# Two layers on one core: latent scores of four heads at once on four banks, rounds of exponentials and masks, and new second-layer stages

## The chip, the core and the metric

The kernel runs on one of the eight cores of a Trainium2 chip. The core's engines run their own instruction streams and meet at semaphores: TensorE (PE, matmuls, a 128x128 array), VectorE (DVE), ScalarE (ACT), GpSimd (POOL) and SyncE (SP, which issues most DMAs). Matmuls write to PSUM; here it is split in two tiles of four banks of 512 fp32 columns each, `pA` and `pD`. All arithmetic is fp32. The metric is the device time of one execution in microseconds; lower is better.

## The reference, cut to what matters

```python
x = L0_attn_x                                    # (8, 512, 256)
xn = layernorm(x)
s = retention(xn)                                # 4 heads, chunks of 64
g = silu(local_ffn(xn))                          # DEPTH = 2 layers, below
x = x + s * g
xn = layernorm(x)
s = latent_attention(xn)                         # 16 heads, below
g = silu(moe(xn))                                # 8 experts, top 2, F = 1024
return x + s * g

def local_layer(x):                              # twice
    h = shift_token(x)                           # half of the channels one token back
    q, k, v = split(h @ wqkv)                    # 8 heads of 64
    q, k = xpos(l2norm(q) * qs, l2norm(k) * ks)
    x = x + attention(q, k, v, window=128) @ wo
    h = layernorm(shift_token(x)) * lg + lb
    a, g = split(h @ w1 + b1)
    return x + (a * gelu(g)) @ w2 + b2

def latent_attention(x):                         # per sequence of 512 tokens
    c_q, c_kv = x @ W_DQ, x @ W_DKV              # 64 latent channels
    Q = [c_q @ W_UQ, rope(c_q @ W_QR)]           # 16 heads of 16 + 8
    K = [c_kv @ W_UK, rope(x @ W_KR)]            # the 8 rotary rows shared by all heads
    scores = clip(Q @ K.T, -80, 80)              # causal
    return softmax(scores / sqrt(24)) @ (c_kv @ W_UV) @ W_O
```

## The kernel before

**Stages.** B = 8 sequences, two local layers, so 16 items; `stages()` yields k = -1 to 15. A stage finishes item k (output projection, feed-forward) and starts item k + 1 (q, k, v, scores, probabilities). Stages 0 to 7 also do retention of sequence k; stages 8 to 15 (the upper stages) also do the latent attention of sequence b = k - 8. Stage 15 has no item k + 1. After the last stage comes the mixture of experts: 71 tiles of 128 rows, with the last sequence's remaining latent work threaded in.

Inside a stage each engine follows an order written out by hand: the stage's start (`out_projection`, transposes), a loop over t (four token tiles: `qk_product`, `v_product`), a loop over c (six chunks of the hidden width: `up_projection`, `gelu`, `gate_up`), and a loop over u (eleven steps: local scores, exponentials, transposes, values, and `down_projection` at u = 1).

**PSUM as rings.** `ring_a_jobs` and `ring_d_jobs` list, in program order, what goes to `pA` (mostly emptied by ScalarE) and `pD` (emptied by VectorE). `bank_ring` gives each job the next one or two of four banks; TensorE waits until the last job in those banks has been emptied, and the engine that empties them works in the same order. An order change on one engine must be made on all.

**Latent attention of sequence b.** `latent_projections` makes the latent rows and the shared key. `keys_queries(b, g)` serves four heads (group g): one matmul of 512 columns for keys, two for queries (plain and partner rows); VectorE multiplies the two by cosine and sine (L1727, L1728) and GpSimd adds them (`query_sum`, L1460). Each head has its own 32 partitions of `QT` and `KT`. `latent_scores(b, w, rounds)` handles a pair of heads w, in three rounds of key tiles (512 columns; 384 and 128; 256), each round a job of two banks, one per head. `clipped` (L1735) moves a round to one of three slots in `pairs_space`, `latent_exp` (L1270) exponentiates the whole pair, 2560 columns, in one instruction, `causal` (L1466, L1467, L1469) multiplies the diagonal blocks by a triangle, and `latent_values` multiplies with the values of a group. `by_token` divides by the row sum. Pairs 0 to 3 run in the u loop of stage 8 + b, pairs 4 to 7 in the next stage, in its t loop and at its first c.

**Other names.** `shifted_stats` on VectorE needs rows that SyncE moves from `cur` one token down, after `attention_out` has added the output projection. `rotary_parts` (L1615 to L1620), `scale_qk` (L1624), `head_norms` (L1450) and `rotary_sum` (L1446) prepare q and k. The router of sequence b - 1 is a run of small VectorE steps (L1762 to L1782) at c = 0; `scatter_rows` (L1480) sends rows to the experts. L703 is the helper of all projections; in the upper stages `x_tm`, the residual input, lies in the same space as `attn`, and the hidden chunks `hT` and two gates `gl` lie in the third slot of the pairs.

## Time and profile before

| | |
|---|---|
| median of 3 runs | 3048.02 us (3040.27 to 3054.22) |
| profiled execution | 3047.79 us, span 3045.9 us |
| TensorE busy | 2770.7 us, 91% |
| VectorE, ScalarE, GpSimd busy | 1627.9, 1213.3, 1077.0 us |
| mean granted TensorE clock | 0.963 of full |
| stages 9 to 14 | 156.82 to 162.89 us each |
| mixture of experts | from 2424.26 us to the end |

A row of a timeline gives the start from the span's start, the duration, engine, line, operation, output<-input, shapes and count, and in brackets the idle time of that engine just before and what ended it. PE rows count an fp32 matmul twice, since it is issued as two instructions. Neighbouring PE rows overlap at their ends, so the distance between two starts is the better measure. A window row lists the busy time of each engine in a stretch, then the granted clock as a share of 2.4 GHz, then the DMA engines' share and rate.

### The profile page before, as it was taken

The page shows a single profiled execution, that of the slowest core. Times are in us where ns is not written, and L with a number is a line of the kernel's source. Part 1 is how long each engine was busy: PE and PEld are TensorE (multiplying, and loading weights), DVE is VectorE, ACT ScalarE, POOL GpSimd, SP SyncE. Part 2 cuts the span into 40 slices and gives each one's busy share as a digit, 9 for nine tenths or more (in the row PEclk, how much of TensorE's full clock was granted, in tenths as well). Part 3 has the DMA queues.
Part 4 walks back from the last instruction along what each step waited for, and adds up shares of the span by engine and source line. Part 5 has one row for each costly group of instructions (what it writes and reads, how often), then busy time and mean ns, then how long its engine had stood idle before and what let it go on. Part 6 is the DMA issues. An engine that isn't in the chain of part 4 may idle for free.

```text
span 3045.9 us, 42333 instructions
## 1 busy us (share of the span) xinstructions
PE 2770.7 (91%) x15646; PEld 1863.9 (61%) x15646; DVE 1627.9 (53%) x3890; ACT 1213.3 (40%) x2265; POOL 1077.0 (35%) x767
## 2 busy tenths in 40 slices
PE   6999999999999899999989898999988899999992
PEld 3565656556565656555555555555554488999992
DVE  6656566575656456676676768585754520000003
ACT  4444444535344444444444544444543232222221
POOL 5423243343423233353444535353532321111113
PEclk8999999999999999999999999999998799999996
DMA  3000000000001011001010101010000367999886
GB/s 134 11 23 17 25 28 25 15 25 15 25 22 46 25 40 59 20 5 49 4 49 4 49 4 42 11 39 15 29 15 31 132 233 268 343 357 344 326 325 206
DMA packets 85767, 261.72 MB, mean 86 GB/s; under 512 B 10653, under 2 KB 49901, under 8 KB 66877
## 3 DMA queue, kind: packets, MB, share of 16 engines
q1 hardware_dynamic: 79084, 241.25, 21.9%
q0 software_dynamic: 6480, 17.77, 1.5%
q8 instruction: 128, 2.10, 0.3%
q14 instruction: 75, 0.61, 0.1%
HBM read 210.68 MB, written 44.11 MB: 84 GB/s over the span
## 4 chain that ended last, share of the span: by engine, by line
PE 73%; DVE 12%; issue 4%; DMA 4%; POOL 3%; ACT 3%; SPq 1%; POOLq 0%; DVEq 0%; ACTq 0%
PE s_pD L703 20%; PE s_pA L703 17%; PE s_pD L1155 7%; PE s_pA L1140 6%; PE s_pD L860 3%; PE s_pA L753 3%; PE s_pD L775 3%; PE s_pA L762 3%; DMA s_w_w<-rows_s 3%; DVE s_pairs L1735 2%; PE s_pA L742 2%; DVE s_qk L1634 2%; PE s_pA L870 2%; ACT s_qk L1209 1%; PE s_pD L941 1%
## 5 line engine op out<-in xcount | busy, mean ns | idle before, releaser
L1456 POOL TENSOR_TENSOR s_qk<-s_qk,s_rrec 128x1024 f32<-128x1024 f32 (+1 forms) x128 | 215.7, 1685 | 578.0 <-DVE s_rrec L1640 577.9
L1209 ACT ACTIVATE s_qk<-s_qk,s_mx 128x256 f32<-128x256 f32 (+1 forms) x512 | 239.9, 469 | 341.0 <-DVE s_mx L1634 340.3
L703 PE MATMUL s_pA<-s_w_wqkv,s_curT 128*128 128x512 f32 x768 | 354.3, 601 | 5.6 <-ACT s_curT L1185 3.7
L703 PEld LDWEIGHTS s_pA<-s_w_wqkv,s_curT 128*128 128x128 f32 x768 | 142.4, 191 | 176.6 <-issue 163.1
L1735 DVE TENSOR_SCALAR s_pairs<-s_pD 128x1024 f32<-128x1024 f32 (+1 forms) x192 | 194.4, 1038 | 103.9 <-PE s_pD L860 101.1
L2086 DVE COPY s_w_wo<-s_pD 128x256 f32<-128x256 f32 x71 | 30.0, 423 | 409.6 <-PE s_pD L1126 409.6
L1555 POOL DMA_INDIRECT acc_s<-s_w_w,s_sq x71 | 68.3, 962 | 458.9 <-ACT s_w_w L1397 451.6
L1450 POOL TENSOR_TENSOR s_rinv<-s_ssq,s_half 128x16 f32<-128x16 f32 x64 | 207.5, 3242 | 5.1
L860 PE MATMUL s_pD<-s_mixer 32*128 32x512 f32 (+3 forms) x1024 | 186.4, 477 | 23.6 <-DVE s_pairs L1735 18.5
L1446 POOL TENSOR_TENSOR s_qk<-s_qk,s_rot 128x1024 f32<-128x1024 f32 x64 | 150.5, 2351 | 135.5 <-DVE s_qk L1617 135.4
L703 PE MATMUL s_pA<-s_zT,s_w_w 128*120 128x512 f32 (+1 forms) x384 | 186.7, 609 | 1.1 <-ACT s_zT L1225 1.1
L1634 DVE CUSTOM_DVE_ANT_0 s_qk<-s_pA,s_maskw 128x256 f32<-128x256 f32 (+1 forms) x512 | 167.9, 385 | 31.2 <-PE s_pA L753 30.7
L1270 ACT ACTIVATE s_pairs<-s_pairs 128x2560 f32<-128x2560 f32 x64 | 149.7, 2338 | 87.3 <-DVE s_pairs L1735 87.2
L703 PE MATMUL s_pD<-s_zT,s_w_w 128*120 128x512 f32 (+1 forms) x384 | 181.7, 596 | 0.0
L860 PEld LDWEIGHTS s_pD<-s_mixer 32*128 32x128 f32 x1024 | 91.6, 193 | 130.6 <-issue 84.4
L1414 POOL TENSOR_TENSOR s_rs<-s_ve,s_half 128x4 f32<-128x4 f32 x40 | 41.1, 1026 | 363.9 <-DVE s_ve L1596 363.9
L762 PE MATMUL s_pA<-s_ident,s_qk 128*128 128x128 f32 x896 | 129.8, 287 | 40.3 <-issue 23.7
L753 PE MATMUL s_pA<-s_qkT 64*128 64x256 f32 (+1 forms) x1024 | 131.7, 380 | 29.9 <-DVE s_mx L1634 14.7
L1191 ACT COPY s_qk<-s_pA 128x1024 f32<-128x1024 f32 x64 | 64.6, 1010 | 217.2 <-PE s_pA L703 217.2
L762 PEld LDWEIGHTS s_pA<-s_ident,s_qk 128*128 128x128 f32 x896 | 99.2, 144 | 83.8 <-issue 58.1
L703 PEld LDWEIGHTS s_pD<-s_zT,s_w_w 128*120 128x120 f32 (+1 forms) x384 | 69.1, 180 | 98.6 <-issue 97.9
L1397 ACT ACTIVATE s_w_w<-s_pD,s_w_w 128x256 f32<-128x256 f32 x71 | 33.6, 473 | 236.8 <-PE s_pD L1155 236.8
(276 smaller groups left out, 5922.9 us busy)
## 6 DMA issues: line engine op xcount, KB each, us to landing
s_qkT<-in_m_w SPq DMA_DIRECT2D x48, 1024.0 KB, 5.2
s_v_tm<-in_m_w SPq DMA_DIRECT2D x24, 1024.0 KB
s_rot<-in_m_w SPq DMA_DIRECT2D x24, 1024.0 KB, 5.1
s_w_wqkv<-in_m_w SPq DMA_DIRECT2D x23, 1024.0 KB
s_qk<-in_m_w SPq DMA_DIRECT2D x23, 1024.0 KB, 6.1
s_w_w<-rows_s SPq DMA_DIRECT2D x71, 129.0 KB
s_cur<-in_x SPq DMA_DIRECT2D x8, 512.0 KB, 3.5
xn_s<-s_cur SPq DMA_DIRECT2D x8, 512.0 KB, 2.8
```

What stands on the lines that cost most here:

```text
L703: last = nc.tensor.matmul(out, lhs(c), rhs(c), start=(c == 0), stop=(c == n - 1))
L753: last = nc.tensor.matmul(ps[:, place(i) * 256 + lo * P:(place(i) + 1) * 256], qkT[r, h // 2, tile_cols(t)], qkT[r, 4 + h // 2, (t - 1 + l ...
L762: last = nc.tensor.transpose(ps[:, (2 * i + k) * P:(2 * i + k + 1) * P], prob[w % 3][:, i * 256 + k * P:i * 256 + (k + 1) * P], ident[:])
L860: last = nc.tensor.matmul(ps[:, 512 * i + col:512 * i + col + T - kt * P], KT[rows, g % 2, tile_cols(kt)], QT[rows, g % 2, kt * P:T], star ...
L1140: last = nc.tensor.matmul(m_ph[u % 2][:, f * P:(f + 1) * P], m_w1[u % NW][:, c * F + f * P:c * F + (f + 1) * P], m_xT[:, u % 2, c * P:(c + ...
L1155: last = nc.tensor.matmul(m_py(w), m_hT[w % 2][:, f * P:(f + 1) * P], m_w2[w % NW][:, f * D:(f + 1) * D], start=(f == 0), stop=(f == FC - 1))
L1209: last = nc.scalar.activation(pi, pi, ACT.Exp, scale=-1.0, bias=mx[:, u, i:i + 1], accum_out=rsum[:, u, i:i + 1])
L1446: nc.gpsimd.tensor_tensor(qk[:, t, :], qk[:, t, :], rot[:, t % 2, :], ALU.add)
L1450: nc.gpsimd.tensor_tensor(rinv[:, t, :], ssq[:, t, :], half[:], ALU.pow).then_inc(rinv_rdy, 1)
L1456: nc.gpsimd.tensor_tensor(pi, pi, rrec[:, u, :].unsqueeze(2).broadcast_to((P, 4, 256 - lo)), ALU.mult).then_inc(p_rdy, 1)
L1634: last = nc.vector.tensor_tensor_reduce(out=prob[u % 3][:, h], in0=ps[:, h], in1=maskw[:, lo:256], scale=-1.0, scalar=3e38, op0=ALU.add, o ...
L1735: nc.vector.tensor_scalar(Pl[:, w % SLOTS, :, ROUND_AT[r]:ROUND_AT[r] + ROUND_N[r]], ps[:, :, 0:ROUND_N[r]], 80.0, -80.0, ALU.min, ALU.max ...
```

## The change

In stages 8 to 15 the latent work is rearranged; stages -1 to 7 issue the same instructions as before, and the last sequence keeps scores by pair.

- **Scores.** `four_scores(b, g, r)` issues one round of a whole group: four heads, each on its own 32 partitions and its own bank of `pD`, key tile by key tile. It takes two jobs of two banks, and waits for both before it begins.
- **Exponentials and masks** are made per round and pair (`part_exp`, `part_causal`): three ScalarE instructions for a pair in place of one.
- **Queries.** Each head's 32 rows hold 16 plain rows, 8 rotary rows and the 8 partner rows, and the shared key is laid out to match (its rotary rows stand twice). One matmul and one VectorE product with `lqt` make a group's queries; `query_sum` is gone.
- **Stages** are three written-out functions: `lower_stage`, `upper_stage`, `final_stage`. Of a sequence, group 0 and the first round of group 1 stay in the u loop of its stage; the rest of group 1, groups 2 and 3 and all four `by_token` come in the next stage, spread over its t, c and u loops. The router is at c = 1, the ranks at c = 4, and in the next u loop follow `latent_values` 3, the transposes of the attention and the second half of the scatter.
- **Memory.** `x_tm` moves to the third slot of the pairs and is loaded once that slot has been read; `hT` and `gl` move to `sq`, `PT_even` and `z`.

```diff
+            def four_scores(b, g, r):
+                pe.wait_ge(outD, doneD["lq", b, g])
+                ps = [slotD("sc", b, 2 * g + pr, r) for pr in range(2)]
+                for kt, col in ROUNDS[r]:
+                    ends = [nc.tensor.matmul(ps[i // 2][:, 512 * (i % 2) + col:512 * (i % 2) + col + T - kt * P], KT[32 * i:32 * i + 32, g % 2, tile_cols(kt)],
+                                             QT[32 * i:32 * i + 32, g % 2, kt * P:T], start=True, stop=True) for i in range(4)]
+                ends[1].then_inc(mmD, 1)
+                ends[3].then_inc(mmD, 1)
...
             def keys_queries(b, g):
                 pe.wait_ge(outD, doneD["lat", b])
                 ps = slotD("kc", b, g)
                 pq = slotD("lq", b, g)
-                nc.tensor.matmul(pq[:, 0:T], W["lWqk"][0:LAT, 0, g, :], latT[0:LAT, :], start=True, stop=True)
-                nc.tensor.matmul(ps[:, 0:T], W["lWqk"][LAT:P, 0, g, :], latT[LAT:P, :], start=True, stop=True).then_inc(mmD, 1)
-                nc.tensor.matmul(pq[:, T:2 * T], W["lWqk"][0:LAT, 1, g, :], latT[0:LAT, :], start=True, stop=True).then_inc(mmD, 1)
+                nc.tensor.matmul(ps[:, 0:T], W["lWqk"][LAT:P, g, :], latT[LAT:P, :], start=True, stop=True).then_inc(mmD, 1)
+                nc.tensor.matmul(pq[:, 0:T], W["lWqk"][0:LAT, g, :], latT[0:LAT, :], start=True, stop=True).then_inc(mmD, 1)
...
+            def part_exp(b, w, r):
+                act.wait_ge(outD, doneD["sc", b, w, r])
+                ph = Pl[:, w % SLOTS, :, ROUND_AT[r]:ROUND_AT[r] + ROUND_N[r]]
                 nc.scalar.activation(ph, ph, ACT.Exp, scale=1.0 / SQ24).then_inc(lexp, 1)
...
             def queries(b, g):
                 ps = take("lq", b, g)
-                if g:
-                    dve.wait_ge(lq_rdy, LG * b + g)
-                nc.vector.tensor_tensor(rm[:, 0, :], ps[:, 0:T], W["lcos"], ALU.mult)
-                nc.vector.tensor_tensor(rm[:, 1, :], ps[:, T:2 * T], W["lsin"], ALU.mult).then_inc(outD, 1)
+                nc.vector.tensor_tensor(QT[:, g % 2, :], ps, W["lqt"], ALU.mult).then_inc(outD, 1)
```

The c loop of an upper stage on TensorE, with the diff's lines in full, and behind it that on VectorE:

```diff
+                for c in range(NHC):
+                    gate_projection(k, c)
+                    if s.mid and c == 2:
+                        latent_values(b - 1, 2)
+                    if s.mid and 2 <= c < 5:
+                        four_scores(b - 1, 3, c - 2)
+                    if c in (3, 4):
+                        head_transposes(k + 1, c - 1)
+                    up_projection(k, c)
+                    if c == 0:
+                        head_transposes(k + 1, 1)
+                    if s.mid and c == 0:
+                        by_token(b - 1, 1)
+                        keys_queries(b - 1, 3)
+                    if s.mid and c == 4:
+                        ranks(b - 1)
+                        by_token(b - 1, 2)
```

```diff
+                for c in range(NHC):
+                    if s.mid and 2 <= c < 5:
+                        four_clipped(b - 1, 3, c - 2)
+                    gate_up(k, c)
+                    if s.mid and c == 0:
+                        by_token(b - 1, 1)
+                        keys_queries(b - 1, 3)
+                    if c == 0:
+                        scale_qk(k + 1, 2)
+                    if s.mid and c == 1:
+                        router(b - 1)
+                    if c == 1:
+                        scale_qk(k + 1, 3)
```

How TensorE's rows move in the c loop of a middle stage, first before, from the second chunk on (L703 are the projections, gate to `s_pA` and up to `s_pD`; L870 the latent values; L742 the transposes of q and k; L860 the scores):

```order
L860 MATMUL s_pD<-s_mixer 128x256 x2
L703 MATMUL s_pA<-s_zT,s_w_w 120x512 x2
L703 MATMUL s_pD<-s_zT,s_w_w 120x512 x2
L703 MATMUL s_pA<-s_zT,s_w_w 120x512 x2
L703 MATMUL s_pD<-s_zT,s_w_w 120x512 x2
L703 MATMUL s_pA<-s_zT,s_w_w 120x512 x2
L703 MATMUL s_pD<-s_zT,s_w_w 120x512 x2
```

And now (L771 projections, L947 latent values, L936 scores, L810 transposes):

```order
L771 MATMUL s_pA<-s_zT,s_w_w 120x512 x2
L771 MATMUL s_pD<-s_zT,s_w_w 120x512 x2
L771 MATMUL s_pA<-s_zT,s_w_w 120x512 x2
L947 MATMUL s_pA<-s_pairs,s_mixer 32x512 x4
L947 MATMUL s_pA<-s_pairs,s_mixer 32x384 x4
L947 MATMUL s_pA<-s_pairs,s_mixer 32x256 x4
L947 MATMUL s_pA<-s_pairs,s_mixer 32x128 x4
L936 MATMUL s_pD<-s_mixer 128x512 x4
L771 MATMUL s_pD<-s_zT,s_w_w 120x512 x2
L771 MATMUL s_pA<-s_zT,s_w_w 120x512 x2
L936 MATMUL s_pD<-s_mixer 128x384 x4
L936 MATMUL s_pD<-s_mixer 128x128 x4
```

Three chunks of up-projections ran in a row, each on one bank; now a round of scores on four banks stands ahead of the up-projection of the third chunk, and another ahead of that of the fourth.

ScalarE in the same c loop, before (L1252 the gelu, L1202 the copies of transposed q and k, L1270 the exponential of a pair, L1274 the latent values' copy):

```order
L1252 ACT_TABLE_LOAD
L1252 ACTIVATE s_pairs<-s_pA,s_w_b 120x512
L1202 COPY s_qkT<-s_pA 128x8x128
L1270 ACT_TABLE_LOAD
L1270 ACTIVATE s_pairs<-s_pairs 128x2560
L1252 ACT_TABLE_LOAD
L1252 ACTIVATE s_pairs<-s_pA,s_w_b 120x512 x3
L1274 COPY s_mixer<-s_pA 128x512
```

And now, from the third chunk on (L1413 the gelu, L1440 the exponentials by round, L1363 the copies):

```order
L1440 ACT_TABLE_LOAD
L1440 ACTIVATE s_pairs<-s_pairs 128x2x512 x2
L1413 ACT_TABLE_LOAD
L1413 ACTIVATE s_z<-s_pA,s_w_b 120x512
L1363 COPY s_qkT<-s_pA 128x8x128
L1440 ACT_TABLE_LOAD
L1440 ACTIVATE s_pairs<-s_pairs 128x2x512 x2
L1413 ACT_TABLE_LOAD
L1413 ACTIVATE s_z<-s_pA,s_w_b 120x512
```

Gelu and exponential now alternate three times, with a table load at each turn: eight loads in a middle stage, where there were four.

## Rows read from the trace of the kernel before

**Rows 1.** Windows by stage: length; busy (count) of PE, PEld, DVE, ACT, POOL; clock; DMA.

```profile
1181.85:1317.46 135.61, 124.89 (x639) 76.92 (x638) 85.68 (x192) 59.09 (x117) 53.23 (x32) 0.95 0.10 35
1317.46:1480.35 162.89, 149.67 (x826) 88.80 (x825) 111.69 (x250) 73.26 (x128) 74.28 (x54) 0.95 0.07 25
...
1795.91:1952.74 156.83, 142.47 (x826) 84.47 (x825) 111.05 (x251) 73.45 (x128) 74.31 (x54) 1.00 0.07 26
...
2274.83:2424.26 149.43, 121.70 (x509) 65.12 (x509) 81.85 (x205) 41.22 (x41) 44.76 (x50) 0.77 0.14 49
2424.26:3045.90 621.64, 551.39 (x3752) 502.96 (x3752) 91.39 (x252) 151.44 (x241) 103.34 (x95) 0.95 0.82 303
```

**Rows 2.** Windows of three parts of the stage k = 12.

```profile
1795.91:1879.35 83.44, 78.33 (x384) 40.97 (x383) 62.56 (x118) 38.90 (x42) 44.69 (x30) 1.00 0.03 11
1879.35:1908.55 29.20, 22.15 (x131) 17.58 (x129) 20.86 (x75) 14.21 (x50) 10.41 (x9) 1.00 0.30 108
1908.55:1952.74 44.19, 41.99 (x314) 25.92 (x315) 27.63 (x61) 20.34 (x37) 19.21 (x16) 1.00 0.00 1
```

**Rows 3.** Lines by form, TensorE, k = 12: count | busy us, mean ns | idle before.

```profile
L860 PE MATMUL s_pD<-s_mixer 32*128 32x512 f32 x32 | 9.0, 637 | 0.7 <-DVE s_pairs L1735 0.7
...
L842 PE MATMUL s_pD<-s_mixer 64*128 64x512 f32 x8 | 4.1, 589 | 0.0
```

**Rows 4.** Timeline, TensorE, k = 12: start us, us, line, [idle before].

```profile
1816.13 1.99 PE L860 MATMUL s_pD<-s_mixer 32*128 32x512 f32 x12
1818.06 3.70 PE L703 MATMUL s_pA<-s_w_wqkv,s_curT 128*128 128x512 f32 x8
1821.69 0.70 PE L860 MATMUL s_pD<-s_mixer 32*128 32x256 f32 x4
...
1859.81 1.88 PE L703 MATMUL s_pD<-s_zT,s_w_w 128*120 128x512 f32 x4
...
1865.05 2.36 PE L870 MATMUL s_pA<-s_pairs,s_mixer 128*32 128x512 f32 x32
...
1872.15 0.60 PE L878 MATMUL s_pD<-s_ident,s_mixer 128*128 128x128 f32 x4
...
1876.89 1.04 PE L714 MATMUL s_pA<-s_ident,s_mixer 128*128 128x128 f32 x8
...
1903.29 1.99 PE L703 MATMUL s_pD<-s_mixer,s_curT 128*128 128x256 f32 x8
```

**Rows 5.** Lines by form, VectorE, k = 12 (columns as in rows 3).

```profile
L1728 DVE TENSOR_TENSOR s_mixer<-s_pD,s_mixer 128x512 f32<-128x512 f32 x4 | 2.7, 680 | 0.0
```

**Rows 6.** Timeline, VectorE, k = 12 (columns as in rows 4).

```profile
1814.93 0.29 DVE L1591 BATCH_NORM_STATS2 s_stat<-s_cur 128x6 f32<-128x128 f32 x1 [1.14 <-DMA s_z<-s_cur]
...
1815.78 0.69 DVE L1735 TENSOR_SCALAR s_pairs<-s_pD 128x512 f32<-128x512 f32 x1
1817.38 2.35 DVE L1735 TENSOR_SCALAR s_pairs<-s_pD 128x1024 f32<-128x1024 f32 x2 [0.91 <-PE s_pD L860]
1819.65 1.28 DVE L1615 TENSOR_TENSOR s_rot<-s_qk,s_w_fS 128x512 f32<-128x512 f32 x2
...
1824.58 0.68 DVE L1735 TENSOR_SCALAR s_pairs<-s_pD 128x512 f32<-128x512 f32 x1
...
1858.66 1.22 DVE L1624 TENSOR_TENSOR s_qk<-s_qk,s_rinv 128x1024 f32<-128x1024 f32 x1 [1.55 <-POOL s_rinv L1450]
1859.80 0.18 DVE L1762 TENSOR_REDUCE s_rt<-s_rt 128x4 f32<-128x32 f32 x1
...
1864.96 1.41 DVE L1674 SCALAR_TENSOR_TENSOR s_pairs<-s_pD,s_w_b,s_pairs 120x512 f32<-120x512 f32 x2
```

**Rows 7.** Timeline, ScalarE, k = 12 (columns as in rows 4).

```profile
1816.72 2.34 ACT L1270 ACTIVATE s_pairs<-s_pairs 128x2560 f32<-128x2560 f32 x1
...
1859.50 1.28 ACT L1252 ACT_TABLE_LOAD   x1
```

**Rows 8.** Waits of TensorE, k = 12: total us, times, longest.

```profile
PE s_pD L703 <- ACT s_zT L1261: 2.4, 1, 2.4
```

1134 lines of the change are left out of this document (715 added, 419 removed).

## The prediction, made before the changed kernel had run

> **What bounds the kernel now.** I read the windows by stage first [rows 1], then the three parts of one undisturbed stage [rows 2], then TensorE's and VectorE's timelines in it. Stages are counted by the k of the code; the six from 9 to 14 have the same work and are called middle stages. The reader is to see that a middle stage at full clock takes 156.83 us, of which TensorE is busy 142.47 and VectorE 111.05 [rows 1]. TensorE is the longer engine, so that work taken from it looks like time won. The parts say otherwise [rows 2]: up to the down-projection (83.44 us) TensorE is busy 78.33, and VectorE 62.56; in the next 29.20 us, until the latent projections, both wait for each other; in the last 44.19 us TensorE is busy 41.99 and VectorE only 25.92.
>
> In the first part VectorE is nearer its limit than its share tells. `shifted_stats` waits for SyncE's moved rows until 1814.93, which is 19.0 us into the stage [rows 6]. From the end of these statistics (1815.78) to the end of the router (1864.96) VectorE is one chain of 49.2 us with few gaps [rows 6]. TensorE keeps busy beside it since it has projections of q, k, v and hidden chunks that need one bank each.
>
> **Cost of a round of scores.** A pair of heads takes 1.93 us for its first two rounds (1816.13 to 1818.06) and about 0.63 for the third (0.70 with its tail) [rows 4]: 2.56 us. One instruction of 512 columns shows 637 ns, but 32 of them fill 9.0 us, 281 ns each [rows 3], so the two heads lie side by side. If four do so as well, a group costs what a pair costs, and 2.56 us are saved per group; if not, nothing. That is the bound on both sides, 0 to 2.56; I take 2.5, because two heads in separate rows and banks already overlap in full and the four are also separate in both. 7 sequences x 4 groups = 28 groups: 0 to 72 us of TensorE. The dropped query matmul is 8 instructions in 4.1 us a stage, 1.0 us a group [rows 3]; 32 groups: 32 us. So TensorE loses about 13.5 us of work in a middle stage. VectorE loses one product of 0.68 us a group (2.7 a stage) [rows 5], GpSimd the sums, which lie in a stage in which it is busy 74.31 of 156.83 us [rows 1].
>
> The Trainium skill (TensorE: Matmul & The Clock Gate, Measured speedup vs the span model) gives 3.07 times the rate for four row tiles of K = 32 and N = 512, not 4. By it a group would take 4/3.07 = 1.3 times what a pair takes here and save 1.8 us, not 2.5. No row here shows four at once.
>
> **First part of a middle stage, recounted.** What VectorE does between the end of the statistics and the release of the third chunk's up-projection, by its own code order:
>
> - Before, the chain of 49.2 us has four pairs' narrow rounds (0.60 apart) and three pairs' wide ones (2.27, 1817.38 to 1819.65) [rows 6]: 9.2 us of clips.
> - Now it has a narrow round of a group (1.2), two wide ones (2 x 2.27), another narrow one (1.2): 6.9 us; two key and query steps of 1.4 (two products of 0.68 [rows 5]), 2.8; one more `gate_up`, 0.7. The four `rotary_parts` (4.93 each, 1819.65 to 1824.58), four `scale_qk` and the router (5.16, 1859.80 to 1864.96) stay [rows 6]. 49.2 - 9.2 + 6.9 + 2.8 + 0.7 = 50.4; without the 2.5 us of gaps in the old chain (0.91 and 1.55 of them in the rows) 47.9.
> - Behind it now stands the first clip of group 3's first round, 1.2 us: only then is a bank free for the up-projection of chunk 2, because a round of four heads holds all four banks. Before, that matmul needed one bank and was three chunks ahead of the router.
>
> Release: 19.9 + 47.9 + 1.2 = 69.0 us into the stage at best, 71.5 with the old gaps; I take 69. Before, it ran at 1859.81, 63.9 us [rows 4]. From there to the down-projection were 19.5 us. Of these the latent values of group 3 (2.3), a `by_token` (0.5) and the attention's transposes (1.3 with the gap) go elsewhere [rows 4], and there come a `by_token` (0.5), a wide and a narrow round (1.6), and waits of about 1.2, where a chunk must wait for the clip of the round before it. ScalarE now turns between gelu and exponential four times more, 1.28 us each [rows 7], 5.1 us a stage at most on the path and nothing at least; I put 0.3 there, since a chunk's two projections (3.4 us of TensorE) cover a load and a gelu. The 1.2 lies between nothing and 4, one clip and its gate for each of three rounds. 19.5 - 4.1 + 0.5 + 1.6 + 1.2 + 0.3 = 19.0. The down-projection starts 88.0 us into the stage in place of 83.4: **4.5 later**, though TensorE has 6.7 us less to do there (3.4 of scores, 2.3 and 1.0).
>
> **Second part**, from the down-projection to the latent projections, 29.2 us. It gains latent values (2.3), a `by_token` (0.5) and the attention's transposes, and loses the second half of the latent output (1.9, which goes behind) [rows 4]. In it stands a chain of VectorE and ScalarE (gated sums, norm, one more block of local scores, copies) that TensorE awaits at its end, 2.4 us [rows 8]. What is put ahead of the chain adds its 2.8 us; what stands inside is hidden by it, and 0.7 comes off. **+2.1**.
>
> **Third part**, 44.2 us, TensorE nearly always busy: real gain. Three groups of keys and queries (2.0 each) become two (1.0): -4.0. Four pairs (10.2) become a group and one wide round (2.5 + 1.0): -6.7. A `by_token` goes, -0.5; the half output comes, +1.9. Against that, ScalarE, busy 20.34 us of this part [rows 2], has one latent exponential of 2.34 us [rows 7] cut in pieces of which each waits for its clip and delays the copy behind it; bounds 0 and 4, and I take +1.3. Together **-8.0**.
>
> Middle stage: +4.5 + 2.1 - 8.0 = -1.4; six of them, -8. Stage 8 has no sequence behind it; it has the third part's gain without the half output (-9.9 of its 135.61), of which I take -9. Stage 15 (149.43 us, clock 0.77 [rows 1]) has TensorE waiting for VectorE already and gets more clips: before 4 pairs' (11.5), now a wide and a narrow round and two groups' (3.5 + 2 x 5.7 = 14.9); against that stand fewer matmuls: 0. One query matmul in the last part (621.64 us, not otherwise touched): -1. Sum: -18. Against the profiled execution's 3047.8 us (0.2 below the median, so they count as one): **3030 us**.
>
> A rule against the change, and for this sum, is in the skill (TensorEngine Tiling (Array Packing), PSUM Bottleneck): tiling speeds up TensorE and not the emptying of PSUM, which can become the bottleneck. By the rows it does: a wide round of a group takes TensorE about 1 us and VectorE 2.27.
>
> **Rivals.**
>
> 1. *TensorE stays the bound everywhere.* For it: TensorE's 142.47 of 156.83. Against it: the chain of 49.2 us. If VectorE runs ahead (the chain stretched in the old kernel by GpSimd's work beside it, and now less), the first two parts fall with TensorE's work, by 6 - some 8 us a stage better than I say: 6 x 8 = 48, and 5 more in stage 15: 2977.
> 2. *The four banks and the clock, slower.* Rounds that take all of `pD` make TensorE idle in pieces: my middle stage has it busy 129 of 155 us, 83%, and stage 15, with 81%, was granted 0.77 of the clock; stages with 91 to 92% got 0.95 and 1.00 [rows 1]. If the clock falls to half for 20 of 155 us in places where TensorE is needed, its work there takes 10 us longer, of which the waits take back some: +7.5 a stage, 6 x 7.5 = 45: 3075. It decides from about 3 us a stage on (3048).
> 3. *The moves cancel.* The gain of the third part is used up in every stage, -1.4 becomes +1: 3044.
>
> That the change doesn't do what it says (four heads not side by side): then the third part gains 4 us less and the first is the same, since VectorE sets it: about +20, inside the cases above.
>
> **Numbers.** What a measurement of this kernel can tell from no change is 0.5%, 15 us: below 3033 is faster, above 3063 slower. Forecast 0.43 (own range 3010 to 3050; 0.26 of it below 3033, 0.17 within), rival 1 0.20 (faster), rival 2 0.23 (slower 0.19, within 0.04), rival 3 0.14 (within 0.11, slower 0.03). Faster 0.46, same 0.32, slower 0.22. The range, 2965 to 3082, takes in rivals 1 and 2 and leaves out a case in which all 104 us of TensorE's work show (2944).
>
> **What would show it.** In the profile after: matmuls of a wide round of a group in about 1 us, started within some tens of ns of each other; the up-projection of chunk 2 late, released by a clip; VectorE without gaps from the statistics to that clip; the down-projection 88 us into a middle stage; the last part near 36 us; eight table loads; TensorE's busy time 80 to 105 us lower in all. I am wrong if a middle stage at full clock is below 150 (the chain didn't bind) or above 160, or if the clock falls in most of them.

## Result and the profile after

The changed kernel takes 3069.8 us (median of 6 runs, 3067.07 to 3074.9) against 3047.38 of the kernel before (6 runs, 3040.27 to 3054.22): ratio 1.0079, 95% interval 1.0062 to 1.0096. It is 0.8% slower. I had forecast 3030 us and faster; the range held the time, the sign was wrong.

The page of the changed kernel, its span and its busy times:

```profile
span 3067.5 us, 42290 instructions
...
PE 2700.6 (88%) x15582; PEld 1831.7 (60%) x15582; DVE 1595.5 (52%) x3858; ACT 1268.4 (41%) x2405; POOL 1033.8 (34%) x735
```

TensorE is busy 70 us less than before and the span is 21.6 us longer. The windows by stage (columns as in rows 1) say where: stages 8, 9, 12, 15 and the last part.

```profile
1183.32:1310.64 127.32, 112.57 (x601) 70.27 (x599) 77.45 (x182) 55.71 (x119) 45.87 (x26) 0.97 0.11 38
1310.64:1474.44 163.80, 137.95 (x821) 82.45 (x817) 106.73 (x246) 81.27 (x148) 68.71 (x50) 0.94 0.07 25
...
1802.00:1965.83 163.83, 138.18 (x820) 82.55 (x816) 106.76 (x246) 81.26 (x148) 68.55 (x50) 0.94 0.07 25
...
2293.56:2450.37 156.81, 110.69 (x537) 61.87 (x533) 85.31 (x208) 53.65 (x60) 45.06 (x52) 0.80 0.14 47
2450.37:3067.47 617.10, 549.96 (x3750) 502.73 (x3750) 91.50 (x251) 150.10 (x239) 99.44 (x91) 0.95 0.83 305
```

Against [rows 1]: stage 8 is 8.3 us shorter. The six middle stages together take 982.9 us (1310.64 to 2293.56) instead of 957.4 (1317.46 to 2274.83): +25.5. Stage 15 is 7.4 us longer (156.81 for 149.43) and the last part 4.5 shorter (617.10 for 621.64); what lies ahead of stage 8 adds 1.5. The sum, unrounded, is +21.6.

The middle stages before differed (156.82 to 162.89, granted clock 1.00 to 0.95); now all six take 163.8 or 163.9 at 0.94. A granted clock between 0.5 and 1 is a mean of stretches at 1.2 and at 2.4 GHz, so about 20 us of each stage ran at the lower level (2 x 0.06 x 163.8). The three parts of k = 12, for [rows 2]:

```profile
1802.00:1892.83 90.83, 77.09 (x372) 39.10 (x368) 64.42 (x116) 47.56 (x57) 40.80 (x27) 0.94 0.05 15
1892.83:1926.89 34.06, 27.59 (x164) 21.05 (x164) 22.12 (x79) 15.21 (x52) 14.98 (x14) 0.85 0.18 63
1926.89:1965.83 38.94, 33.50 (x284) 22.39 (x284) 20.22 (x52) 18.49 (x39) 12.78 (x10) 1.00 0.04 14
```

The reader is to see +7.4, +4.9 and -5.25 us where the forecast said +4.5, +2.1 and -8.0, +7.0 in all. That is against k = 12 of the kernel before, one of its two fastest middle stages; against the mean of its six (159.6 us) the change costs 4.3 us a stage, and six times that is the 25.5. TensorE's timeline in that stage (columns as in rows 4):

```profile
1810.05 1.15 PE L936 MATMUL s_pD<-s_mixer 32*128 32x384 f32 x16
1811.13 3.70 PE L771 MATMUL s_pA<-s_w_wqkv,s_curT 128*128 128x512 f32 x8
1814.76 0.71 PE L936 MATMUL s_pD<-s_mixer 32*128 32x256 f32 x8
1815.40 5.42 PE L771 MATMUL s_pA<-s_w_wqkv,s_curT 128*128 128x512 f32 x12
...
1833.39 1.14 PE L936 MATMUL s_pD<-s_mixer 32*128 32x512 f32 x8 [1.05 <-DVE s_mixer L2007]
1834.46 5.42 PE L771 MATMUL s_pA<-s_w_wqkv,s_curT 128*128 128x512 f32 x12
...
1851.15 1.94 PE L810 MATMUL s_pA<-s_ident,s_qk 128*128 128x128 f32 x8 [5.50 <-DVE s_qk L1908]
...
1871.94 3.09 PE L771 MATMUL s_pD<-s_zT,s_w_w 128*120 128x512 f32 x4 [2.30 <-DVE s_pairs L2016]
```

Four heads do lie side by side: a group's rounds take 1.07, 1.08 and 0.64 us from start to start, 2.79 in all, where a pair took 2.56 [rows 4]. A group saves 2.3 us of TensorE, where I had taken 2.5. An estimate from the Trainium skill's 3.07 (TensorE: Matmul & The Clock Gate, Measured speedup vs the span model) would have been 1.8, less than was measured.

The last row shown is the up-projection of chunk 2, released by a clip 69.9 us into the stage (forecast 69.0). The row ahead of it is a wait that no term of the prediction holds: the head transposes stand 5.5 us. The profile names VectorE's scale as the releaser, but they need the scale of tile 0 alone, which ran at 1838.08 and was done at 1839.3; they waited for a bank of `pA`. ScalarE's timeline shows who held it:

```profile
1848.60 1.06 ACT L1440 ACTIVATE s_pairs<-s_pairs 128x1024 f32<-128x1024 f32 x1 [3.82 <-DVE s_pairs L2016]
1849.56 0.57 ACT L1359 COPY s_v_tm<-s_pA 128x512 f32<-128x512 f32 x1
1850.03 1.94 ACT L1386 ACTIVATE s_zT<-s_pA,s_w_ln 128x256 f32<-128x256 f32 x4
```

A latent exponential waits 3.8 us for its clip, and the copy of v and the scaled copies of `zT`, which free the banks, are queued behind it. VectorE in turn waits for the narrow round behind the transposes (first row), and 16 us later comes the clip that frees chunk 2:

```profile
1854.36 1.29 DVE L2016 TENSOR_SCALAR s_pairs<-s_pD 128x512 f32<-128x512 f32 x2 [3.53 <-PE s_pD L936]
...
1870.67 2.35 DVE L2016 TENSOR_SCALAR s_pairs<-s_pD 128x1024 f32<-128x1024 f32 x2
```

Windows of this stage show what follows the waits: the granted clock (third column from the right) is 1.00 until the long wait, 0.65 in and behind it, 1.00 again, 0.79 around the wait for chunk 2, and 0.60 behind the waits of the second part.

```profile
1840.00:1846.00 6.00, 3.94 (x28) 2.43 (x28) 5.97 (x6) 4.31 (x5) 4.58 (x4) 1.00 0.00 0
1846.80:1853.60 6.80, 2.45 (x12) 2.08 (x16) 4.03 (x4) 4.78 (x8) 5.67 (x4) 0.65 0.00 0
1860.00:1870.00 10.00, 9.64 (x56) 3.48 (x54) 9.35 (x28) 3.21 (x5) 4.39 (x2) 1.00 0.03 8
1870.70:1874.10 3.40, 2.16 (x4) 0.93 (x5) 2.32 (x3) 2.11 (x2) 0.73 (x1) 0.79 0.21 75
1911.60:1921.90 10.30, 6.96 (x40) 5.12 (x41) 8.76 (x31) 3.67 (x12) 2.96 (x3) 0.60 0.28 103
```

### The profile page after: what moved, and what is told of

Read it like the earlier page. It is cut to its first block, busy times and chain, and to the rows that moved or that the text cites. A ratio compares the mean times of both kernels' runs of the same rounds, so it can differ in the third digit from the quotient of the medians.

```text
span 3067.5 us, 42290 instructions
## 1 busy us (share of the span) xinstructions
PE 2700.6 (88%) x15582; PEld 1831.7 (60%) x15582; DVE 1595.5 (52%) x3858; ACT 1268.4 (41%) x2405; POOL 1033.8 (34%) x735
## 4 chain that ended last, share of the span: by engine, by line
PE 66%; DVE 17%; DMA 5%; issue 5%; ACT 3%; SPq 3%; POOL 1%; POOLq 0%; DVEq 0%; ACTq 0%
PE s_pD L771 20%; PE s_pA L771 14%; PE s_pD L1316 7%; PE s_pA L1301 7%; PE s_pA L821 3%; PE s_pA L830 3%; PE s_pD L843 2%; DVE s_pairs L2016 2%; DMA s_w_w<-rows_s 2%; DVE s_qk L1918 2%; ACT s_qk L1370 2%; PE s_pA L810 2%; PE s_pD L936 1%; DMA s_z<-s_cur 1%; DVE s_rot L1899 1%
## 5 line engine op out<-in xcount | busy, mean ns | idle before, releaser
L771 PE MATMUL s_pA<-s_w_wqkv,s_curT 128*128 128x512 f32 x768 | 353.2, 600 | 5.6 <-ACT s_curT L1346 3.7
L771 PEld LDWEIGHTS s_pA<-s_w_wqkv,s_curT 128*128 128x128 f32 x768 | 142.7, 191 | 180.2 <-issue 162.9
L1440 ACT ACTIVATE s_pairs<-s_pairs 128x1024 f32<-128x1024 f32 x168 | 151.6, 914 | 191.1 <-DVE s_pairs L2016 188.7
L771 PE MATMUL s_pD<-s_zT,s_w_w 128*120 128x512 f32 (+1 forms) x384 | 191.7, 623 | 21.6 <-DVE s_pairs L2016 21.6
L771 PE MATMUL s_pA<-s_zT,s_w_w 128*120 128x512 f32 (+1 forms) x384 | 188.9, 616 | 1.2 <-ACT s_zT L1386 1.2
L821 PE MATMUL s_pA<-s_qkT 64*128 64x256 f32 (+1 forms) x1024 | 140.5, 397 | 30.0 <-ACT s_PT_even L1380 13.4
L771 PEld LDWEIGHTS s_pD<-s_zT,s_w_w 128*120 128x120 f32 (+1 forms) x384 | 68.0, 182 | 115.7 <-issue 82.9
L1717 POOL TENSOR_TENSOR s_pairs<-s_pairs,s_tri 128x256 f32<-128x256 f32 x112 | 90.0, 817 | 138.8 <-ACT s_pairs L1440 138.6
L821 PEld LDWEIGHTS s_pA<-s_qkT 64*128 64x128 f32 x1024 | 93.9, 200 | 68.5 <-issue 34.1
```

The source lines that it names most:

```text
L771: last = nc.tensor.matmul(out, lhs(c), rhs(c), start=(c == 0), stop=(c == n - 1))
L821: last = nc.tensor.matmul(ps[:, place(i) * 256 + lo * P:(place(i) + 1) * 256], qkT[r, h // 2, tile_cols(t)], qkT[r, 4 + h // 2, (t - 1 + l ...
L1440: nc.scalar.activation(ph, ph, ACT.Exp, scale=1.0 / SQ24).then_inc(lexp, 1)
```

## Experiments

My first theory (A): the new order makes waits among VectorE, ScalarE and TensorE that eat what TensorE saves. Rivals: the clock takes the gain back (B, G); TensorE is the bound everywhere (C); rounds of four bring nothing (D). The runs are numbered: e4 is "the fourth run" of the texts, e11 the eleventh. Ratios are to the kernel before on the same chip, with 95% intervals. That kernel's median went from 3042.0 to 3050.4 us from chip to chip, so runs of different groups (e1 to e4; e5 to e8; e9 to e12; e13 to e16) are compared by their ratios and not by their times. Stage lengths come from one profiled execution each.

### One part alone: the query split

The kernel before with `WIDE` without `"lq"`, the table `lqt`, and

```diff
-                nc.tensor.matmul(pq[:, 0:T], W["lWqk"][0:LAT, 0, g, :], latT[0:LAT, :], start=True, stop=True)
...
-                nc.tensor.matmul(pq[:, T:2 * T], W["lWqk"][0:LAT, 1, g, :], latT[0:LAT, :], start=True, stop=True).then_inc(mmD, 1)
+                nc.tensor.matmul(pq[:, 0:T], W["lWqk"][0:LAT, g, :], latT[0:LAT, :], start=True, stop=True).then_inc(mmD, 1)
```

> The kernel before, its order untouched, with the query split in rows alone (one query matmul, one product with the table, no sum on GpSimd). Theory A (the new order and its waits cost the time, the parts by themselves pay): 3 groups a stage lose 1.0 us of TensorE in the third part, where it is the bound, the fourth lies in the first part, which VectorE sets but where VectorE loses 0.7 too; 3 to 4 us a stage in 7 stages: 3020 to 3027 us against the before of 3047. Rival B (work taken from TensorE anywhere lowers its clock and comes back as time): no gain, 3040 or more, and a lower granted clock.

Measured: 3052.37 us, 1.0014 (1.0002 to 1.0027). Theory A failed here: 32 us less work on the longer engine brought nothing. TensorE was busy 2768.4 us, 2.3 less than before, at a clock of 0.956 against 0.963. Part of the saved work also came back as waiting. In the third part of k = 12 TensorE stands idle 3.9 us for 2.2 before, most of it because the latent scores now wait for VectorE's product of the queries (waits of TensorE: what waited, releaser, total us, times, longest; first this run, then before):

```profile
PE s_pD L859 <- DVE s_mixer L1709: 1.7, 2, 0.9
```

```profile
PE s_pD L860 <- DVE s_mixer L1728: 0.4, 2, 0.2
```

Then the same kernel with the one query matmul issued twice:

> The kernel before with the query split alone (first run: 3052 us, no gain, though TensorE has 32 us less to do), and the one query matmul issued twice, so that TensorE has the old work again while VectorE and GpSimd keep what they gained. Theory G (the clock took the gain back): 3030 to 3050 us, no slower than with one matmul, and the third parts of the middle stages back at a clock of 0.95 to 1.00 from 0.88 to 0.95. Theory H (clock of no account, TensorE the bound in the third part): plus 1 us for each of 31 groups, 3075 to 3085.

Measured: 3044.1 us, 0.9985 (0.9973 to 0.9997); the two intervals are apart. With 31 matmuls more the kernel is 0.3% faster. The third part of k = 12, first with one query matmul, then with two (windows, as rows 2):

```profile
1917.09:1963.80 46.71, 42.82 (x308) 27.34 (x309) 25.84 (x58) 20.34 (x37) 15.40 (x13) 0.93 0.01 3
```

```profile
1913.18:1957.24 44.06, 41.90 (x314) 26.60 (x315) 26.04 (x58) 20.23 (x37) 15.40 (x13) 1.00 0.00 1
```

Less work, a lower clock and more time; the six middle stages took 161.1 us on average with one, 159.6 with two and 159.6 before. (The execution profiled with one matmul was 7 us slower than its median, so the ratios say better how large the effect is: 0.3%.) With two matmuls the wait for the product is gone too and TensorE is idle 2.2 us again, so the pair of runs shows that the removed work was worth nothing, and it doesn't split that between the clock and the wait.

### Do four heads need to be interleaved, and what is their overlap worth

```diff
+                for pr in range(2):
+                    for kt, col in ROUNDS[r]:
+                        for i in (2 * pr, 2 * pr + 1):
```

> The changed kernel with all its order, banks and waits, but in a round of four heads the matmuls of the first pair are issued ahead of those of the second, so that four heads never lie side by side. Theory A (VectorE and ScalarE set the first and second part of a middle stage): TensorE gets back about 2.5 us a group, 70 us in all, but time shows it only in the third part and stage 8 (about 3 us each of 7), some of it is taken back by a better clock: 3085 to 3095 us. Rival C (TensorE is the bound everywhere): plus 60 to 70, 3130 or more. Rival D (the rounds of four bring nothing): 3070.

Measured: 3077.17 us, 1.0094 (1.0075 to 1.0113), no different from the changed kernel. My edit was no test of the overlap: two of the three rounds have one key tile and kept their order, and the third took 1.10 us all the same:

```profile
1809.37 1.17 PE L938 MATMUL s_pD<-s_mixer 32*128 32x384 f32 x16
1810.47 1.98 PE L771 MATMUL s_pA<-s_w_wqkv,s_curT 128*128 128x512 f32 x4
```

So the test was made again with rows shared:

```diff
-KT[32 * i:32 * i + 32, g % 2, tile_cols(kt)], QT[32 * i:32 * i + 32, g % 2, kt * P:T]
+KT[32 * (i % 2):32 * (i % 2) + 32, g % 2, tile_cols(kt)], QT[32 * (i % 2):32 * (i % 2) + 32, g % 2, kt * P:T]
```

> The changed kernel, where heads 2 and 3 of a round of four read the rows of keys and queries of heads 0 and 1 (their scores are other numbers than the reference's), so that they can't lie side by side with them on TensorE; banks, waits and order are those of the changed kernel. Theory A: a wide round then takes 2 us in place of 1.08, a group some 2.5 us more; in the third part and stage 8, without other cover, 3 us more each, in the first part half of it hidden behind VectorE: 3085 to 3120 us. Rival D (four heads do not overlap more than two; the first two waves run as pairs anyway): rounds as long as before, 3070.

Measured: 3091.43 us, 1.0149 (1.0112 to 1.0185). The round takes 1.94 us:

```profile
1819.38 2.00 PE L936 MATMUL s_pD<-s_mixer 32*128 32x384 f32 x16
1821.32 3.70 PE L771 MATMUL s_pA<-s_w_wqkv,s_curT 128*128 128x512 f32 x8
```

TensorE is busy 2763.5 us, 62.9 more than with the overlap, and the time is 0.7% (22 us) longer: of what the overlap saves on TensorE a third shows. By subtraction (not by a run of its own) the new order without overlap costs some 41 us over the query split (1.0149 against 1.0014), and the overlap gives half of it back.

### Rounds of four in the third part only

The kernel before, query split, `QUADS = {6: (0, 0), 7: (0, 1), 9: (1, 0), 10: (1, 1)}` in the u loop, third rounds at u = 8 and 10.

> The kernel before with the query split, and rounds of four heads only in the third part of the stages 8 to 14 (groups 0 and 1, spread over the steps u = 6 to 10); the first and second part keep their pairs and their order. Theory A: TensorE is the bound in the third part and VectorE idle there: 2 groups x 2.5 us = 5 us a stage, 35 us beside the query split: about 2990 us. Rival E (what is late at the end of the third part, the clips and the two exponentials of 2.34 us of group 1, delays the copies at the start of the next stage): the gain comes back there, 3015 or more.

Measured: 3104.68 us, 1.0182 (1.0165 to 1.0199): the worst but one. Rival E had the sign, but neither the place nor the size. It put the loss at the start of the next stage, where it is 1.9 us a stage (first part 86.7 us on average, 84.8 in e1). Most of it lies in the third part itself: 52.6 us in place of 44.2 before and 46.7 in e1, at 0.86 of the clock, with TensorE idle for 12.2 us, mostly in waits for VectorE's clips and products:

```profile
1939.94:1992.56 52.62, 40.42 (x309) 25.36 (x309) 26.14 (x60) 17.91 (x40) 12.82 (x10) 0.86 0.00 1
```

### ScalarE's order

```diff
-                    if s.mid and t > 1:
-                        part_exp(b - 1, 4, t - 2)
                     v_copy(k + 1, t)
...
                     if s.mid and t == 2:
-                        part_exp(b - 1, 5, 0)
+                        four_exp(b - 1, 2, 0)
...
                 norm_in("zT", k, 1, zT, W["ln"])
                 if s.mid:
-                    part_exp(b - 1, 5, 1)
+                    four_exp(b - 1, 2, 1)
```

> The changed kernel, where ScalarE alone has another order in the t loop: the exponentials of group 2's first two rounds stand behind the copies of v and behind the scaled copies of zT, not ahead. Theory A (head transposes wait 5.5 us a stage for banks that ScalarE's copies hold, since these stand behind an exponential that waits for a clip; VectorE then idles 3.5 us ahead of the narrow clip): that wait falls to 2 us or less, the up-projection of chunk 2 comes 3.5 us earlier, the half clock at 47 us into the stage goes: 3.5 to 6 us a stage, 3035 to 3049 us. Rival F (the scale of tile 1 on VectorE, behind two clips, is what the transposes wait for, as the profile's releaser says): no change, 3065 to 3070.

Measured: 3057.37 us, 1.0027 (1.0012 to 1.0041), two thirds of the loss gone by an order on ScalarE alone. The wait for transposes is 0.8 us, and the releaser named before, VectorE's scale, was not it: they now run 3 us ahead of the scale of tile 1. The first part of k = 12 takes 88.0 us, 4.6 more than before, where the forecast said 4.5:

```profile
PE s_pA L810 <- issue: 0.8, 1, 0.8
```

Then the same with another order of the final tanh on ScalarE and of the row ends on VectorE (the diff shows what is new against the fourth run):

```diff
+                    if u == 1:
+                        final_tanh(b, range(0, 2))
                     if s.mid and u == 1:
                         values_out(b - 1, 3)
                     if u == 1:
-                        final_tanh(b)
+                        final_tanh(b, range(2, NT))
...
-                    if s.mid and u == 1:
-                        row_ends(b - 1, 1)
...
                         ffn_out(k, 0)
+                        if s.mid:
+                            row_ends(b - 1, 1)
```

> The changed kernel with the copies ahead of group 2's exponentials (fourth run, 3057 us), and in the second part the first two of the four final tanh ahead of the copy of group 3's values (in the eighth run all four stood ahead, and the copy waited for the feed-forward's second half, with that the turned attention: slower), the second row ends behind the feed-forward output. Theory A: 1.5 to 2 us less a stage than the fourth run, 3043 to 3050 us, level with the kernel before. Rival J (TensorE at its lower clock sets the second part): as the fourth run, 3057.

Measured: 3052.47 us, 1.001 (0.9995 to 1.0025): level with the kernel before, and not clearly faster than the fourth run. Middle stages 160.5 us (161.1 in the fourth run), their first part 87.3.

```profile
1791.97:1879.23 87.26, 76.23 (x372) 38.32 (x368) 65.21 (x116) 47.91 (x57) 41.16 (x27) 0.96 0.05 16
1879.23:1913.49 34.26, 27.78 (x164) 21.15 (x165) 21.30 (x79) 15.32 (x52) 15.20 (x14) 0.85 0.17 62
```

```diff
                         values_out(b - 1, 2)
-                        four_exp(b - 1, 3, 0)
...
-                    if s.mid and c in (3, 4):
-                        four_exp(b - 1, 3, c - 2)
+                if s.mid:
+                    for r in range(3):
+                        four_exp(b - 1, 3, r)
```

> The changed kernel, where ScalarE computes all exponentials of group 3 behind the last gelu of the stage, not between its gelus: the four extra table loads and the two behind them fall away (6 x 1.28 us a stage). Theory A: the loads lie beside the waits for clips in the chunk loop, so that the down-projection comes at most 1 us earlier; but 5 us of exponentials now stand ahead of the local ones, and the values of group 3 come later: 3065 to 3085 us. Rival I (the table loads set the pace of the chunk loop): the first part of 90.8 us falls by 2 us or more, 3050 or less.

Measured: 3114.09 us, 1.0221 (1.0202 to 1.024). The first part is the same without the loads (90.65 us for 90.83), so they are not on the path; the values of group 3 then wait 5.3 us for masks in the second part (windows of the two parts, then the wait):

```profile
1823.24:1913.89 90.65, 78.06 (x372) 39.15 (x368) 64.44 (x116) 36.16 (x47) 35.79 (x22) 0.94 0.05 15
1913.89:1954.97 41.08, 30.21 (x164) 21.57 (x164) 21.86 (x79) 18.75 (x57) 20.02 (x19) 0.79 0.15 52
```

```profile
PE s_pA L947 <- POOL s_pairs L1717: 5.3, 1, 5.3
```

```diff
-                    if s.mid and u == 1:
-                        values_out(b - 1, 3)
                     if u == 1:
                         final_tanh(b)
+                    if s.mid and u == 1:
+                        values_out(b - 1, 3)
...
-                    if s.mid and u == 1:
-                        row_ends(b - 1, 1)
...
                         gated_sum(b, 0)
+                        if s.mid:
+                            row_ends(b - 1, 1)
```

> The changed kernel, where in the second part of a middle stage VectorE writes the second row ends behind its first gated sum (not ahead of the feed-forward output, where it waits 2.25 us for the landing of the first scatter), and ScalarE computes the final tanh ahead of its copy of group 3's values (1.5 us). Theory A: VectorE's chain in the second part gets 3 to 4 us shorter, the part falls from 34.0 to 31 to 32 us, 3050 to 3058 us. Rival J (the second part is set by TensorE, with latent values and down-projection put there, and its half clock): no change.

Measured: 3085.16 us, 1.013 (1.0111 to 1.0149), a miss: the copy of group 3's values, behind all four tanh, came late, and `by_token` waited for it:

```profile
PE s_pD L955 <- ACT s_mixer L1444: 2.1, 1, 2.1
```

### The clock in the changed kernel

```diff
+                for again in range({2: 1, 3: 2}.get(t, 0) if B + 1 < b < ITEMS else 0):
+                    project(ps[:, 0:512], shifted_lhs(t), lambda c: W["wqkv"][:, c, 1024:1536], DC)
...
-                for i in range(4):
+                for i in [0, 1, 2, 3] * (1 + 2 * (u == 3 and B + 1 < b < ITEMS)):
```

> The changed kernel, where TensorE computes some results more often than needed, in the places where it stands idle in a middle stage: v of tile 2 twice, v of tile 3 three times (ahead of the wait of 1.8 and of 5.5 us), the local scores of step 3 three times (ahead of the waits of 1.35 and 2.7 us). That is 7.4 us more work a stage, 44 us in all, and the results are the same. Theory G (the lower granted clock behind these waits costs time of its own): the half-clock spells at 47 and 112 us into the stage shrink or go, a middle stage falls from 163.8 to 158 to 161, 3035 to 3060 us: more work, less time. Theory H (the waits alone cost the time; what runs at half clock lies beside VectorE's chain): no change within 0.2%, or slower by 1 to 3 us a stage, 3070 to 3085.

Measured: 3064.3 us, 1.0063 (1.0043 to 1.0082). 44 us more work cost nothing (the gain in time is within the intervals). Busy time rose by 29 us only, the mean clock from 0.953 to 0.962, and the middle stages fell from 163.8 to 162.2 us on average, in an execution that was the fastest of six. The first and second part of k = 12, and behind them the second part of k = 11:

```profile
1798.14:1886.40 88.26, 80.10 (x385) 39.99 (x381) 64.56 (x116) 47.46 (x57) 40.82 (x27) 0.98 0.05 16
1886.40:1920.56 34.16, 28.51 (x181) 22.16 (x181) 21.76 (x79) 15.22 (x52) 14.98 (x14) 0.90 0.18 63
...
1724.82:1757.58 32.76, 27.36 (x180) 21.51 (x180) 21.96 (x79) 15.10 (x52) 14.98 (x14) 0.95 0.20 65
```

The first part falls to 88.3 us in k = 12 (89.5 in k = 11). The second takes the same at 0.90 as at 0.85, and 1.3 us less at 0.95, where the third part that follows took 1.6 more at 0.96.

What half clock costs is plainest from the up-projection of chunk 2 to the down-projection, where TensorE hardly waits. The same 92 instructions, in the changed kernel and then in the eleventh run's, where no half clock falls on them:

```profile
1871.94:1892.83 20.89, 20.02 (x92) 9.80 (x92) 11.37 (x29) 16.91 (x17) 5.16 (x6) 0.92 0.00 1
```

```profile
1860.04:1879.23 19.19, 18.32 (x92) 9.21 (x92) 11.37 (x29) 16.91 (x17) 5.16 (x6) 1.00 0.01 1
```

It is 19.2 us at 1.00 in e5 and e12 too, and 20.6 to 20.9 at 0.92 or 0.93 in e4 and e13.

The eleventh run's kernel with the fill above (v of tile 2 and the scores alone) and the diff of the next section:

> The eleventh run's kernel, with the exponentials of the third part one step later (tenth run), and with the clock held: v of tile 2 computed twice and the local scores of step 3 three times in a middle stage, with the same results. Theory G: the gains add, 6 stages at 155 to 157 us as in the kernel before and stage 8 shorter by 8: 3025 to 3042 us, faster than the kernel before by 0.2 to 0.7%. Theory H: no better than the eleventh run, or slower by the added work, 2 us a stage.

Measured: 3052.84 us, 1.0019 (1.0003 to 1.0036). Once the 5.5 us wait is gone, filling brings no more: second part 34.30 us at 0.90, in the eleventh run 34.26 at 0.85. Theory G's gain doesn't come; but the fill raised the mean clock from 0.955 to 0.959 only, which makes this a weak test of it.

### The third part

```diff
-                    if 6 <= u < 9:
-                        four_exp(b, 0, u - 6)
+                    if 7 <= u < 10:
+                        four_exp(b, 0, u - 7)
```

> The changed kernel, where in the third part ScalarE's exponentials of group 0 and GpSimd's masks stand one step u later, so that they never wait for a clip of the same step, and the copy of the turned probabilities is not behind such a wait. Theory A (ScalarE's pieces cost the third part 3 us a stage, the waits of 1.4 and 1.1 us for a copy): third part from 38.94 to 36 to 37.5 us, 3050 to 3062. Rival K (the exponentials themselves, not their waits, hold the copies; or the values of group 0 now come late at the stage's end): no change, or slower by up to 2 us a stage.

(GpSimd's `four_causal` moves with it.)

Measured: 3071.21 us, 1.0073 (1.0045 to 1.0101). Third part 38.94 us as in the changed kernel, and TensorE waits for the same copies as long (2.5 us for `s_rot`):

```profile
PE s_pD L843 <- ACT s_rot L1380: 2.5, 2, 1.4
PE s_pD L936 <- DVE s_sq L1929: 1.7, 3, 0.8
```

So the exponentials' waits are not what holds the copies.

```diff
                         local_scores(k + 1, u)
+                    if u == 10:
+                        latent_values(b, 0)
...
                         four_scores(b, 1, 0)
-                        latent_values(b, 0)
```

> The fourteenth run's kernel, and in the third part TensorE's latent values of group 0 stand ahead of the local values of step 10, whose copy of turned probabilities they cover (a wait of 1.1 us), and ahead of the first round of group 1. Theory N (in the third part each us less of TensorE's work uncovered the latency of a copy, so that waits grew from 2.2 to 5.4 us): third part from 38.9 to 37.5 to 38 us, 6 to 9 us less than the fourteenth run. Rival: the next stage's out-projection waits for the later local output, no change.

Measured: 3057.03 us, 1.0037 (1.0026 to 1.0049). The wait of 1.1 us is gone, but the third part takes 39.5 us, 0.5 longer: the next stage's output projection, which ends it and waited for nothing in the fourteenth run, now waits 1.5 us, as the rival said:

```profile
1958.36 7.14 PE L771 MATMUL s_pD<-s_w_wo,s_sq 128*128 128x256 f32 x32 [1.47 <-DVE s_pairs L2017]
```

Theory N's gain did not come, and what sets this part stays open.

### Who sets the first part

```diff
-                    if s.mid and t == 1:
-                        by_token(b - 1, 0)
...
-                    if s.mid and t > 1:
-                        four_scores(b - 1, 2, t - 2)
                     v_product(k + 1, t)
+                    if s.mid and t == 1:
+                        by_token(b - 1, 0)
+                    if s.mid and t > 1:
+                        four_scores(b - 1, 2, t - 2)
...
-                if s.mid:
-                    four_scores(b - 1, 2, 2)
...
                     gate_projection(k, c)
+                    if s.mid and c == 0:
+                        four_scores(b - 1, 2, 2)
```

> The eleventh run's kernel (3052 us), and on TensorE alone another order: what waits for a bank of the rounds of four (a by_token, the first two rounds of group 2, the last of it) stands behind a v or gate projection that has its bank already. Theory L (VectorE's chain from the statistics to the clip ahead of chunk 2 sets the first part, as the prediction says): the up-projection of chunk 2 stays at 67.8 to 68.5 us into the stage and the down-projection at 86.5 to 87.3; what is gained is a better clock at most: 3043 to 3053 us. Theory M (TensorE's order, with bank waits ahead of work that needs none, sets it): the waits of 2.2, 1.05 and 2.4 us go, the first part falls by 3 to 5 us: 3022 to 3035 us.

Measured: 3055.14 us, 1.0042 (1.0029 to 1.0056). That is slower than the eleventh run (1.001, its interval ends at 1.0025). Up-projection of chunk 2 at 67.4 us into the stage (1796.98; 68.1 in the eleventh run), first part 88.3: the waits moved and none of the time went.

```profile
1864.38 3.67 PE L771 MATMUL s_pD<-s_zT,s_w_w 128*120 128x512 f32 x4 [2.66 <-DVE s_pairs L2016]
```

```diff
-                    if s.mid and c == 1:
-                        router(b - 1)
...
+                    if s.mid and c == 2:
+                        router_probabilities(b - 1)
+                        router_pick(b - 1, 0)
+                    if s.mid and c == 3:
+                        router_pick(b - 1, 1)
+                        router_weights(b - 1)
```

> The thirteenth run's kernel, and on VectorE the router (3.8 us) behind the first clip of group 3, in two pieces behind the gates of chunks 2 and 3, where VectorE waits anyway. Theory L (VectorE's chain sets the release of chunk 2): the up-projection of chunk 2 comes 3.5 us earlier, at 64 to 65 us into the stage, the down-projection 2 to 3.5 us earlier: 3028 to 3040 us. Theory M (TensorE sets it): no change from the thirteenth run.

Measured: 3052.04 us, 1.0026 (1.0012 to 1.0041). The router's 3.8 us off VectorE's chain bring the matmul 1.3 us forward (1857.69 in a stage from 1791.54), and the first part is 87.35 us, as in the eleventh run (87.26); the intervals of this run and the thirteenth overlap:

```profile
1857.69 1.98 PE L771 MATMUL s_pD<-s_zT,s_w_w 128*120 128x512 f32 x4 [1.39 <-DVE s_pairs L2016]
```

Neither L nor M. In the thirteenth run VectorE came to that clip without a gap; now it gets there early and waits 2.5 us for TensorE's round of scores:

```profile
1856.41 2.36 DVE L2016 TENSOR_SCALAR s_pairs<-s_pD 128x1024 f32<-128x1024 f32 x2 [2.47 <-PE s_pD L936]
```

So VectorE's chain and TensorE's own work stood 1.3 us apart here (3.8 less 2.5), and easing one meets the other. The moved router costs some of it again: the up-projection of chunk 4, without a wait in the thirteenth run, now waits 1.8 us for a clip behind it.

```diff
                         four_scores(b - 1, 3, c - 2)
+                    if s.mid and c == 2:
+                        gate_projection(k, 3)
```

> The fifteenth run's kernel, and the gate projection of chunk 3 ahead of the up-projection of chunk 2, which waits 1.9 us for the clip. Theory L: that wait falls to nothing and the down-projection comes 0.5 to 1.5 us earlier: 3 to 8 us less than the fifteenth run. Theory M: no change. Rival: the gelu of chunk 3 then stands ahead of an exponential and its table load, the clips of group 3 wait longer: slower.

Measured: 3058.09 us, 1.0041 (1.0029 to 1.0054), the same as the fifteenth. The up-projection of chunk 2 no longer waits, and that of chunk 4 waits 1.75 us in k = 12. No version beat both kernels but the query split with its matmul doubled, by 0.15%.

## Why the prediction was wrong

The forecast for the whole was -18 us and +21.6 were measured, 39.6 apart. The six middle stages make 33.5 of that (+25.5 for -8), and in k = 12 each of the three parts missed by about 2.8 us. The first of them is explained by experiments and is the step that failed; the other two are open.

- **TensorE's saving.** Right in mechanism and nearly in size: 2.3 us a group for 2.5. Busy time fell by 70 us, which is outside the 80 to 105 I named; with some 20 us of each middle stage at half clock, what is left to do took longer.
- **First part, forecast +4.5, measured +7.4.** This is the step that failed: the forecast counted VectorE's chain without gaps, and of ScalarE it knew only table loads, "0.3". The loads cost nothing (e7). What ScalarE's queue does cost is copies that free banks behind an exponential that waits for a clip: 5.5 us of TensorE idle in each middle stage. Another order on ScalarE gives back 2.7 us a stage (e4), and together with that of the tanh and row ends 3.3 (e11), 20 of the 25.5 us that the middle stages lost. I listed the chain on VectorE from row to row and never asked what stood behind a new wait on ScalarE.
- **The release of chunk 2, 69.9 us for 69.0.** This came close by luck. The chain had a gap of 3.5 us that I had not counted, and without it took 45.0 us for my 47.9. In e4 it has no gap and takes 46.0, and the release comes at 67.4. That VectorE's chain releases chunk 2 is right for e13, where there is no gap ahead of the clip; in e14, with the chain 3.8 us shorter, TensorE's round does.
- **From there to the down-projection, forecast 19.0, measured 20.9.** At full clock the same instructions take 19.2 (e11, e5). The missing term is the clock.
- **Second part, +2.1 for +4.9.** The clock explains 1.3 us of it at most (34.1 us at 0.85, 34.2 at 0.90 and 32.8 at 0.95 in e5). The rest is open.
- **Third part, -8.0 for -5.25.** TensorE's work fell by 8.5 us (41.99 to 33.50), near my 9.3; its waits rose by 3.2 where I had 1.3 for ScalarE's pieces. Those pieces were not the cause (e10). That less work now lies between a transpose and its copy is a guess; e15, meant to test it, moved the wait and did not shorten the part.
- **Stages 8, 15 and the last part.** Stage 8 was right, -8.3 for -9. Stage 15 was not, +7.4 for 0: TensorE waits 5.7 us at its end for the rows of the first expert, 1.6 before, and the rest is open. The last part gave -4.5 for -1, so that the two together look better than they are.
- **Rival 2.** Right in sign and place: full-bank rounds, some 20 us of each stage at half clock. That its 3075 lies near 3070 is luck, since the larger part of the loss is ScalarE's queue: half of the stretch at half clock removed gave 1.6 us a stage (e5). The kernel before had this already, and I read it as noise: k = 9 and k = 12 have the same work and differ by 6.1 us at 0.95 and 1.00 [rows 1].
- **Sign.** ScalarE's order alone doesn't explain it: with it mended, the kernel is still level with the one before and not faster (1.001, 0.9995 to 1.0025). Underneath lies a price that I took for granted, that work taken from TensorE is time where it is busy 42 of 44 us. e1 shows that even the simplest such saving, 1 us a group, comes to nothing here, as a lower clock and as a wait for the product that the removed matmul had hidden.

## What to carry to other kernels

When an instruction in a queue gets a new wait, list what is queued behind it on that engine and whose buffers those free: here two kinds of copies behind one exponential made two thirds of the loss (e4). The releaser that a profile names may have been done long before; a reorder of one engine tells. And before crediting work taken from the busiest engine, look at stages with equal work: if their clock and length differ, the saved time may return as a lower clock, and the cheapest test is to put the removed work back as idle repetition. Compare the waits of the two runs as well, since removed work may have covered one.

## What the runs showed of the hardware

- Four matmuls on separate 32-row tiles and banks overlap whether they are interleaved by head or issued pair after pair (1.08 and 1.10 us a round); sharing rows makes 1.94 (after, e2, e9).
- More TensorE work in the same order made the kernel faster by 0.3% (e6 against e1), and 44 us of repeated matmuls were free in waits (e5).
- The same 92 TensorE instructions took 19.2 us at a granted clock of 1.00 and 20.9 at 0.92 (e11, after), while a part with waits took the same at 0.85 and 0.90 (34.26 us in e11, 34.30 in e12).
- A table load took 1.28 us, and six fewer of them a stage changed the first part by 0.2 us (e7).
